# Second expert layer: routed and sorted in tiles for three chunks, masked densely for the fourth

## The reference, cut to what matters

```
x = x + 0.5 * expert(norm(x))      # L0, first expert layer
x = x + attention0(norm(x))
x = x + 0.5 * expert(norm(x))      # the same weights again: second expert layer
x = x + 0.5 * ternary(norm(x))     # quantised MLP, hidden 512
x = x + attention1(norm(x))
x = x + 0.5 * ternary(norm(x))
```

```
expert_idx = argmax(softmax(x @ Wr.T))
for e in range(8):
    inter += (expert_idx == e)[:, None] * gelu(x @ W1[e] + b1[e])     # 128 -> 512
y = inter @ Wo + bo + x                                               # 512 -> 128
out = layernorm(y) * gamma + beta
```

## Time and profile before

| what | value |
|---|---|
| median of three runs | 1214.37 us |
| profiled execution | 1215.68 us, of which the span is 1213.9 |
| TensorE busy | 1091.9 us, 90% |
| VectorE busy | 1006.6 us, 83% |
| ScalarE busy | 664.6 us, 55% |
| GpSimd busy | 65.8 us, 5% |
| mean granted TensorE clock | 0.975 |
| second expert layer | from 599.1 to 725.9 us of the span |

### The profile page before, as it was taken

The page is one execution under the profiler, slowest core; times in us unless marked ns, Lnnn a source line. Parts: engine busy times, 40 slices in busy tenths (PEclk is TensorE's granted clock), DMA queues, the critical chain, the costliest instruction groups (busy, mean ns, idle before and its releaser), DMA issues.

```text
span 1213.9 us, 34232 instructions
## 1 busy us (share of the span) xinstructions
PE 1091.9 (90%) x14757; PEld 492.3 (41%) x14757; DVE 1006.6 (83%) x2343; ACT 664.6 (55%) x861; POOL 65.8 (5%) x62
## 2 busy tenths in 40 slices
PE   1898976999999999999699987689999999999988
PEld 1455552333333333334345555433333333333436
DVE  8977568999999999886547657799999999998764
ACT  0322222556777777777332214145667777887773
POOL 5111001000000000000100100100000000000000
PEclk9999988999999999999799998899999999999999
DMA  5100034100000000000000000620000000000001
GB/s 158 36 1 1 1 98 117 33 3 2 2 3 2 3 2 3 3 2 3 1 1 2 1 1 1 181 64 3 2 3 2 2 2 2 3 2 3 4 3 35
DMA packets 23555, 24.07 MB, mean 20 GB/s; under 512 B 3134, under 2 KB 21220, under 8 KB 23404
## 3 DMA queue, kind: packets, MB, share of 16 engines
q1 hardware_dynamic: 22252, 18.73, 5.4%
q0 software_dynamic: 1152, 3.15, 1.0%
HBM read 13.20 MB, written 8.39 MB: 18 GB/s over the span
## 4 chain that ended last, share of the span: by engine, by line
PE 55%; DVE 37%; issue 4%; ACT 3%; DMA 1%; SPq 0%; DVEq 0%; ACTq 0%
DVE part_max L1356 25%; PE psum L1215 12%; PE psum L1237 11%; PE psum L443 10%; PE psum L1186 6%; PE psum L467 3%; ACT hidden L1319 2%; PE psum L1201 2%; PE psum L899 2%; PE psum L1243 1%; DVE xn L168 1%; PE psum L1264 1%; DVE norm_v L151 1%; PE psum L914 1%; PE psum L428 1%
## 5 line engine op out<-in xcount | busy, mean ns | idle before, releaser
L1356 DVE TENSOR_REDUCE part_max<-psum 128x1 f32<-128x512 f32 (+3 forms) x1120 | 677.1, 668 | 52.7 <-PE psum L1243 35.3
L1319 ACT ACTIVATE hidden<-psum 128x1024 f32<-128x1024 f32 (+3 forms) x640 | 539.0, 895 | 220.8 <-PE psum L1186 219.7
L1237 PE MATMUL psum<-k_slots,q_slots 128*32 128x512 f16 (+3 forms) x5120 | 389.9, 355 | 31.4 <-DVE part_max L1356 13.5
L1215 PE MATMUL psum<-hidden,v_aug 128*9 128x512 f32 (+3 forms) x2560 | 290.3, 530 | 0.1
L1237 PEld LDWEIGHTS psum<-k_slots,q_slots 128*32 128x32 f16 x5120 | 123.3, 95 | 286.2 <-DVE part_max L1356 193.1
L443 PE MATMUL psum<-parts,w_parts 128*128 128x512 f16 x768 | 179.5, 385 | 1.9 <-DVE parts L839 1.9
L1186 PE MATMUL psum<-q_slots,k_slots 32*128 32x512 f16 (+3 forms) x1472 | 141.3, 328 | 9.6 <-ACT hidden L1319 7.7
L443 PEld LDWEIGHTS psum<-parts,w_parts 128*128 128x128 f16 x768 | 73.6, 99 | 82.4 <-issue 5.7
L587 ACT CAST parts<-psum 128x512 f16<-128x512 f32 x64 | 37.2, 588 | 107.1 <-PE psum L428 107.1
L1243 PE MATMUL psum<-ident_bf,later_keys 128*32 128x128 bf16 (+2 forms) x1408 | 91.5, 250 | 0.0
L1186 PEld LDWEIGHTS psum<-q_slots,k_slots 32*128 32x128 f16 x1472 | 42.0, 91 | 99.7 <-ACT hidden L1319 49.0
(11 more groups left out here) (168 smaller groups left out, 731.4 us busy)
## 6 DMA issues: line engine op xcount, KB each, us to landing
q_slots<-q_rows SPq DMA_DIRECT2D x8, 512.0 KB, 3.8
k_slots<-k_rows POOLq DMA_DIRECT2D x24, 128.0 KB, 4.2
q_rows<-parts SPq DMA_DIRECT2D x18, 128.0 KB, 3.0
k_rows<-parts SPq DMA_DIRECT2D x18, 128.0 KB, 2.8
q_slots<-in_L_ffn_W_dram SPq DMA_DIRECT2D x2, 1024.0 KB, 6.5
k_slots<-k_rows SPq DMA_DIRECT2D x8, 128.0 KB, 4.0
q_slots<-nm_parts SPq DMA_DIRECT2D x64, 4.0 KB
out_dram<-x_res SPq DMA_DIRECT2D x4, 256.0 KB, 2.3
```

Source lines behind the costliest of these rows:

```text
L1215: last = pe.matmul(psum[VW * h:VW * h + DH + 1, O_BANK, off:CH], v_aug[:, j, G * g + h, :], probs[:, (2 * n + h // 2) % NP, h % 2, off:CH] ...
L1237: last = pe.matmul(psum[rows32(m), bank, a * w:(a + 1) * w], q_slots[:, g, qb * P + m * SLOT:qb * P + (m + 1) * SLOT], k_slots[:, G * g + ...
L1319: act.activation(probs[:, tile % NP, :, off:CH], psum[:, bank:bank + 2, off:CH], ACT.Exp, scale=scale).then_inc(exp_done, 1)
L1356: dve.tensor_reduce(part_max[:, step_no[s] % 2, h0:h0 + heads, i, kc], psum[:, bank, 0:heads * w].rearrange("p (a k) -> p a k", a=heads), ...
```

## The change

The second expert layer gets a function of its own, `hybrid_expert_layer`, and a class `Router`. In attention 0 the router takes the chunks 3, 2 and 1 as they complete: `features`, `logits` and `ranks` become ring items in turns 150 to 165, and VectorE computes for each token a row number within its expert's region of 2048 rows in DRAM (`region_dram`, 8 MB, zeroed in the first expert layer). GpSimd scatters the normed rows of each chunk there, four indirect DMAs of 128 rows for a chunk. After attention a table is computed on the chip (how many tiles of 128 rows each expert has, where each starts); SP reads the 20 starts into registers and loads 20 tiles, four in a group. TensorE reads the 20 expert numbers into registers and multiplies each tile with that expert's weights only. Each group's result is normed, scaled with gamma and stored to `sorted_dram`; when all five are stored, GpSimd gathers the rows back into `x_plus`, and the sum with `x_res` is made with the next norm. Chunk 0 is the last of the order and is computed densely as before, behind the tiles; it completes too late in attention to be sorted.

The orders change with it, to 3, 2, 1, 0 for the second expert layer and 3, 1, 0, 2 for the first ternary layer. `Norms` gets `make_piece`: the norms made in attention are cut into six pieces and put into the turns after the chunk is complete (turns 120 to 125 for chunk 3, 144 to 149 for chunk 2, 160 to 162 for chunk 1 in attention 0), three chunks instead of two, in both attentions. In the first ternary layer the projection of attention's first chunk moves behind the last down product, and its low parts behind the last addition.

```diff
+DENSE = 1
+TILES = 20
...
             def make(self, dve, own, scratch, chunk):
+                if self.arrived and chunk in self.arrived:
+                    rows = slice(chunk * BPC, (chunk + 1) * BPC)
+                    dve.wait_ge(self.arrived[chunk], 16 * BPC)
+                    own.wait()
+                    own(dve.tensor_tensor(x_res[:, rows, :], x_plus[:, rows, :], x_res[:, rows, :], ALU.add))
...
+            if router:
+                for turn, kind, n in ((150, "features", 0), (152, "logits", 0), (154, "ranks", 0),
+                                      (157, "features", 1), (159, "logits", 1), (161, "ranks", 1),
+                                      (163, "features", 2), (164, "logits", 2), (165, "ranks", 2)):
+                    tail.setdefault(turn, []).append((kind, n))
...
+                def tiles(n):
+                    if n == 0:
+                        pe.wait_ge(table_ready, 2)
+                    chosen = [pe.value_load(tile_i[0:1, 0, n * BPC + i:n * BPC + i + 1], min_val=0, max_val=E - 1)
+                              for i in range(BPC)]
+                    pe.wait_ge(lo_ready, n + 1)
+                    for t in range(HT):
+                        if n >= 1:
+                            pe.wait_ge(gelu_done, HT * (n - 1) + t + 1)
+                        pe.matmul(psum[:, t, :], b1_parts[:, t * P:(t + 1) * P],
+                                  tile_experts[:, n * BPC:(n + 1) * BPC].rearrange("p (k a) -> p k a", a=1).broadcast_to(
+                                      [P, BPC, P]), start=True, stop=False)
+                        for i in range(BPC):
+                            for wp, xp in ((0, 0), (0, 1), (1, 0)):
+                                weights = w1_parts[:, bass.ds(chosen[i], 1), wp, t * P:(t + 1) * P]
+                                last_m = pe.matmul(psum[:, t, i * P:(i + 1) * P], weights.rearrange("p a i -> p (a i)"),
+                                                   x_parts[:, n % XBUFS, xp, i * P:(i + 1) * P], start=False,
+                                                   stop=(i, wp) == (BPC - 1, 1))
...
+                pe.wait_ge(*released)
+                tile_table()
+                sorted_transposes(0)
+                for n in range(TGROUPS):
+                    tiles(n)
+                    if n == 0:
+                        sorted_transposes(1)
+                        pe.wait_ge(back_ready, 1)
+                        router.transposes(pe, psum[:, PREP_BANK, :], n_last).then_inc(last_on_pe, 1)
+                    if n == 1:
+                        pe.wait_ge(last_on_act, TURNED_ACT)
+                        router.logits(pe, psum[:, PREP_BANK, :], n_last).then_inc(last_on_pe, 1)
+                    if n == 2:
+                        last_choices()
+                    if n + 2 < TGROUPS:
+                        sorted_transposes(n + 2)
+                    if n == TGROUPS - 2:
+                        for e in range(AHEAD_E):
+                            mask_of(e)
+                    if n >= 1:
+                        down(n - 1)
+                for e in range(E):
+                    if e + AHEAD_E < E:
+                        mask_of(e + AHEAD_E)
+                    masked_expert(e)
+                    if e == 2:
+                        down(TGROUPS - 1)
+                last_biases()
+                down(TGROUPS)
...
+                # vector engine
+                tile_table()
+                ways_back()
+                norms.make(dve, own, s1, last)
+                low_part(0)
+                low_part(1)
+                last_low_part()
+                for n in range(TGROUPS - 1):
+                    ...
+                    finish(n)
+                for e in range(AHEAD_E, E - 1):
+                    masked(e)
+                finish(TGROUPS - 1)
+                masked(E - 1)
+                first_back = next_norms.order[0]
+                next_norms.make(dve, own, s1, first_back)
+                finish(TGROUPS)
+                for c in next_norms.order[1:next_given]:
+                    next_norms.make(dve, own, s1, c)
...
+                # gpsimd
+                for n, c in enumerate(sorted_chunks):
+                    pool.wait_ge(router.placed, n + 1)
+                    for i in range(BPC):
+                        b = n * BPC + i
+                        pool.indirect_dma_start(out=region_dram, out_offset=bass.IndirectOffsetOnAxis(place[:, b:b + 1], 0),
+                                                in_=xn[:, c * BPC + i, :], in_offset=None).then_inc(scattered, 16)
+                    add_beta(c)
...
+                for n in range(TGROUPS):
+                    pool.wait_ge(group_moved[n], STORED)
+                pool.wait_ge(back_ready, 2)
+                # then four indirect gathers for each of the chunks 3, 1, 2, in that order
...
+                # sync
+                sp.wait_ge(table_ready, 1)
+                starts = [start_of(k) for k in range(BPC)]
+                sp.wait_ge(scattered, 16 * BPC * len(sorted_chunks))
+                for k, start in enumerate(starts):
+                    load(k, start)
+                for k in range(BPC, TILES):
+                    load(k, start_of(k))
...
-                        following.transposes(pe, 0)
                     if n >= 1:
                         down(n - 1)
+                down(NCH - 1)
                 if following:
+                    following.transposes(pe, 0)
                     following.queries_keys(pe, 0)
-                down(NCH - 1)
...
-        BETWEEN, TURNING = (3, 2, 0, 1), (0, 3, 1, 2)
-        orders = (UP, UP, BETWEEN, TURNING, TURNING, DOWN)
+        TURNING = (0, 3, 1, 2)
+        LATER = (3, 1, 0, 2)
+        orders = (UP, UP, DOWN, LATER, TURNING, DOWN)
```

537 lines of the change are left out of this document (494 added, 43 removed).

## The result

The changed kernel takes 1220.45 us (median of 5 runs, 1219.49 to 1220.91), the kernel before 1214.37 beside it: a ratio of 1.0044, interval 1.0029 to 1.0058. The forecast was 1205, faster: wrong in its sign. The profiled execution spans 1217.8 us, against 1213.9.

A forecast was written before the change was run, and what follows sets the result against it. The prediction took TensorE to bound the changed layer. Its terms, -20.3 + 1 + 3.6 + 5 + 1.5 = -9.2 us against 1215.7, gave 1206.5, hence a median of 1205; forecast range 1198 to 1212 (chance 0.42), widest 1190 to 1226.

The forecast's parts named there:

- part 5: Both attentions: norms in pieces and the router's work lengthen attention 0 by 5 us and attention 1 by 1.5.
- net +3.5, bounds -3 and +10: Attention 0's tail: one wait goes, chunk 1's norm, features and logits come before the last values; 3.5 us more.
- The pieces, +1.5 in my sum: Norms cut into six pieces in crowded attention turns: 1.5 us more a layer, bounds 0 and 4.8 for each norm.
- parts 1 and 2: Second expert layer's tile stage and start: first tile 13.5 us after attention, biases at +91.0, a gain of 28.3 us.
- The pitch: Tile stage: step between 128-column expert matmuls with register-addressed weights, taken as 0.10 us.
- rival (a): Tile stage: register addresses cost nothing, pitch 0.056 us, 10.6 us less: 1195; chance 0.22.
- (b): Tile stage: the sequencer becomes the bound; kernel slower from a pitch of 0.138 us, 1224 at 0.18; chance 0.16.
- Rival (c): Tile stage stays at half clock, its matmuls being short and gapped; costs 8 + 4 us: 1217; chance 0.08.
- part 3: Hand-over to the ternary layer: first low part at +112.7 against +133.0; gives back 8 of the 28.3 us.
- part 4: First ternary layer: another norm with addition, +1 us; attention's first projection moved, +3.6 us before the next attention's loads.
- any loss makes the sum wrong: Whole kernel, closing sign: a gain over 25 us or any loss would show the sum of terms wrong.
- Rival (d): GpSimd's queue: scatters and gathers take 3 us instead of 1.2, delaying first load and gathers: 1213; chance 0.12.

The follow-up runs named there:

- plain_moves: Changed kernel with its 12 indirect scatters and 12 gathers replaced by plain transfers of the same blocks; span 1204.8 us, 0.9938 of the kernel before.
- tile_scatters: Changed kernel with twelve more indirect scatters that nothing waits for, four behind each of the first three tile groups; span 1211.2 us, 0.9967 of the kernel before.
- scatters_held: As router_last, and no scatter starts before the last value matmuls are copied out, beta additions behind all scatters; span 1210.7 us, 0.9967 of the kernel before.
- router_last: Changed kernel with the third sorted chunk's transposes behind attention 0's last value matmuls, logits and ranks behind the last projection; span 1219.8 us, 1.0040 of the kernel before.
- gathers_held: Changed kernel with the eight gathers of chunks 1 and 2 waiting for the last chunk's down product; span 1216.3 us, 0.9994 of the kernel before.
- both_held: Changed kernel with the holds of scatters_held and gathers_held, and the first tile's low part before chunk 0's norm; span 1206.0 us, 0.9953 of the kernel before.
- projection_last: Kernel before with only attention 1's first projection moved behind the ternary layer's last down product, its low parts behind the last sum; span 1212.9 us, ratio 1.0018.
- zero_second: As both_held, with the ternary layer's chunks in the order 3, 0, 1, 2; span 1212.4 us, 0.9974 of the kernel before.
- before_many: Kernel before with 36 indirect scatters that nothing waits for, twelve in attention 0 and 24 in the dense layer, eight in a row; span 1228.4 us, ratio 1.0125.
- after: The changed kernel itself, in its first profile; span 1217.8 us, 1.0044 of the kernel before.
- before_plain: Kernel before with twelve plain 64 KB transfers added on GpSimd at three places in attention 0; span 1215.7 us, ratio 1.0010.
- dense_scatters: Kernel before with twelve indirect scatters that nothing waits for, in three groups of four in the dense expert layer; span 1212.7 us, ratio 0.9997.

## Why the prediction was wrong

The terms against the changed kernel's trace, in the table's stages (measured less forecast):

- **A, attention 0 (part 5): +11.6 us.** The step that failed is the term for the tail, "net +3.5, bounds -3 and +10". Together with the pieces it made "+5 in attention 0"; 16.6 was measured. The pieces, +1.5 in my sum, cost 2.1 from the tenth division to the thirteenth, so they were about right. (My own working, 4.8 us of which 1.7 to 3.1 find idle time, leaves 1.7 to 3.1 a norm for two norms, more than the 1.5 that I took for the layer.) The tail, from the thirteenth division to the end of the attention, is the mis-sized term: +14.8 for +3.5. Stretches of before and of the changed kernel, columns as in the table by stage:

```profile
561.50:599.10 37.60, 28.66 (x499) 13.38 (x495) 21.75 (x74) 20.72 (x31) 5.00 (x4) 0.93 0.01 2
...
563.30:615.70 52.40, 40.65 (x581) 21.73 (x573) 24.90 (x88) 20.98 (x31) 14.15 (x14) 0.80 0.05 16
```

  The same tail took 48.2 us in plain_moves, 44.5 in tile_scatters and 40.0 in scatters_held. So the late signals, which I had not at all, are 4.2 to 7.9 of the 14.8, and even without them the tail was 6.9 to 10.6 over before. (plain_moves lost more: there a VectorE operation of chunk 1's norm, 0.16 us elsewhere, took 1.95 at 593.46, up to the end of a GpSimd addition.) That rest I put down to the third routed chunk in a chain at low clock; it is argued and not shown. The chain of waits of the changed kernel has norm, transposes, logits and only then the last values. The transposes of L261 took 0.60 at full clock, the logits 1.01.

```profile
596.49 1.83 PE psum L1818 x8
...
601.77 1.12 DVE xn L191 x4
...
603.03 1.21 PE psum L261 x4
...
605.10 1.84 PE psum L267 x8
606.94 0.59 PE psum L1818 x8
```

  With the scatters held and the order turned round, the tail is 2.4 over before: no more than I had forecast, but logits and ranks of the third chunk stand behind it there, in B. The order alone (router_last) brought 0.7 in A. The granted clock from 575 to 599 was 0.79 in the changed kernel, 0.85 in plain_moves, 0.96 in scatters_held, 0.98 in tile_scatters and 0.90 in the kernel before. I read from it that the waits cost twice, in themselves and by the clock of what follows, but no run sets the clock alone.

- **B, the start and the tile stage (parts 1 and 2): -6.3 us.** The first tile came at +12.05 (13.5 forecast; the terms that I named add up to 13.15). The pitch was mis-sized: 240 expert matmuls, whose rows (min/median/max ns) stand beside 160 register instructions of 46 ns:

```profile
L1133 PEld LDWEIGHTS psum<-parts,w_parts x240: 95/97/147, 627.8 to 671.1; 128*128 x120
L1133 PE MATMUL psum<-parts,w_parts x240: 217/219/311, 628.1 to 671.2; 128*128 128x128 f16 x120
L1133 PEldq FUSED_REGOPS  x160: 46/46/51, 627.7 to 671.1; - x160
```

  A step of one bias and twelve is 1.08 us, so (1.08 - 0.22) / 12 = 0.072, where I took 0.10 and rival (a) 0.056. The 0.028 less in 240 matmuls are 6.7 us. With the 1.45 of the first tile that is more than the 6.3: some 1.9 us went elsewhere in the stage, whose groups started 8.4, 10.0, 9.8 and 11.0 us apart. Rival (a) was the nearer one; (b), the side I gave the chance of a loss to, did not come near 0.138. Rival (c), half the clock through the stage, didn't come either: from 636 to 700, the second group on, the granted clock was 1.00.

- **C, the hand-over (part 3): +6.6 us.** The add and norm of chunk 3 took 5.65 as said, the finish with the norm behind it 12.6 as said (716.11 to 728.73); chunk 3's rows came 5.0 us behind the biases, not 3.5, and 5.0 us were the late signal. Without it 3.5 to 4.6 come back (gathers_held, tile_scatters, both_held), not all 5.0, since other waits take its place.

- **D (part 4): +0.2.** 4.8 for 4.6, but put down to the wrong half: 0.6 to 0.9 are the moved projection (projection_last), the rest by elimination chunk 0's norm as third and the added sums.

- **E: +0.2; F: +0.9**, within the spread of F.

Together 13.2, which turns -9.2 into the measured +3.9, a loss: by the prediction's own last sign, "any loss makes the sum wrong". That 1220 lies inside the widest range, 1190 to 1226, is luck: what put it there was none of the cases for which that range was made so wide. Rival (d) came nearest in kind: it had GpSimd's queue, but as slow transfers of 3 us (an indirect one took 0.95 at a distance of 1.27; I had taken 1.2). It missed that beside a transfer on GpSimd two engines that have nothing to do with it can wait for the signals of a third. The chance of "slower", 0.30, rested mostly on the sequencer and the clock of the tile stage, and neither came.

**What stays open.** Why TensorE's signals are late beside indirect transfers, and when: the same transfers at the same places had none in tile_scatters, the ranks had one in zero_second and none in both_held, and groups of four had none in the dense layer while groups of eight had. The chip, the layout of tiles and buffers, and the number of transfers alone are out. How the 7 to 11 us that the tail lost without late signals divide between order, clock and VectorE's stall isn't separated either.

## What to carry to other kernels

Before moving routing into an attention, ask of every indirect transfer what waits closely for TensorE while GpSimd issues it, and put it where the readers of TensorE have something in hand (three masks in the dense layer here); a wait in GpSimd's queue did it in scatters_held and both_held. Run a plain transfer in its place first: it costs one edit and gives the price of the form. And when a stage gains and the kernel doesn't, read the granted clock by slices: here the low digits marked the stretches where TensorE waited for others, the attention's tail and the hand-over.

## What the runs showed of the hardware

- Beside an indirect DMA on GpSimd, ScalarE and VectorE may receive TensorE's signals late: 1.7 us (before_many, 656.07), 2.4 (after, 579.28) and 7.2 (after, 716.05) behind the matmul's modelled end. TensorE went on starting matmuls in before_many. Beside plain ones on the same queue there was no such wait (plain_moves, before_plain). The price is nearly the same for 64 rows and 128: 10.8 and 12.0 us for twelve (12.8 in before_many), so 0.9 to 1.1 us an instruction in attention 0.
- An indirect transfer of 128 rows keeps GpSimd for 0.94 (gathers) to 0.97 us (scatters), and one starts 1.25 to 1.29 us after the other; a plain one of the same bytes takes 0.54 (plain_moves).
- VectorE's tensor_scalar of four columns took 3.56 us instead of 0.17 beside three GpSimd additions, 3.70 us together (scatters_held), and one that writes fp16 parts 3.65 instead of 0.67 beside a scatter and two additions (dense_scatters, above). The Trainium skill ("SBUF — State Buffer", SBUF: two separate sides) says that VectorE and GpSimd share a port pair under an exclusive lock, held for a whole instruction. The first case fits in part: the small operation ends with GpSimd's additions, but behind the third of them, where a lock held for one instruction would let it in behind the first. The page also says that TensorE and ScalarE never wait on anyone there, so it doesn't explain the late signals.
